# Slot weights turned in two passes and spread by transfers, a centring matrix, and values weighed in three rounded passes

## What is computed

```python
Q = xn @ Wq + bq                                   # layer 0, per sequence of 512
probs = softmax(Q @ Q.T / sqrt(128));  s = probs @ Q
logits = (xn @ phi_w.T + phi_b).reshape(t, z, 64, 32)
D = softmax(logits, axis=slots);  C = softmax(logits, axis=experts)
X = layernorm(einsum('tznp,tzd->npd', D, xn));  Y = tanh(X) @ expert_w + expert_b
g = silu(einsum('tznp,npH->tzH', C, Y));  x = x + s * g
xn = layernorm(x)                                  # layer 1
h_t = a_t * h_(t-1) + gated_t;  s = rmsnorm(h) @ W_out.T
k = relu(xk @ W_k.T)**2;  r = sigmoid(xr @ W_r.T);  g = silu(r * (k @ W_v.T));  x = x + s * g
```

## Time and profile before

| | |
|---|---|
| runs | 1345.48, 1346.94, 1347.56 us (median 1346.94) |
| the profiled execution | 1348.3 us, its span 1346.2 us |
| PE busy | 1252.0 us (93%) |
| DVE, ACT, POOL busy | 1051.1, 740.2, 814.2 us (78%, 55%, 60%) |
| mean granted clock of TensorE | 0.98 |
| DMA | 167.35 MB, mean 124 GB/s |

### The profile page before, as it was taken

The page is one execution under the profiler, slowest core; times in us unless marked ns, Lnnn a source line. Parts: engine busy times, 40 slices in busy tenths (PEclk is TensorE's granted clock), DMA queues, the critical chain, the costliest instruction groups (busy, mean ns, idle before and its releaser), DMA issues.

```text
span 1346.2 us, 17623 instructions
## 1 busy us (share of the span) xinstructions
PE 1252.0 (93%) x4866; PEld 740.7 (55%) x4866; DVE 1051.1 (78%) x1533; ACT 740.2 (55%) x1459; POOL 814.2 (60%) x768
## 2 busy tenths in 40 slices
PE   6699999999999999998699999999999999999984
PEld 2465555555555555553465555665555565555641
DVE  6899999999999999996455777666776667776653
ACT  2655556556665555653434555555655555655554
POOL 3588989999898898996244454343453344453320
PEclk9899999999999999999799999999999999999997
DMA  6433333333333333333643333333333333333310
GB/s 199 120 139 124 141 128 137 140 125 140 134 131 141 124 140 131 134 141 141 196 133 118 102 125 117 111 125 110 118 123 105 125 118 110 117 110 125 125 32 16
DMA packets 123217, 167.35 MB, mean 124 GB/s; under 512 B 7153, under 2 KB 99313, under 8 KB 122993
## 3 DMA queue, kind: packets, MB, share of 16 engines
q1 hardware_dynamic: 122688, 164.65, 35.5%
q10 hardware_dynamic: 434, 1.59, 0.4%
HBM read 90.71 MB, written 75.50 MB: 123 GB/s over the span
## 4 chain that ended last, share of the span: by engine, by line
PE 37%; POOL 5%; DVE 4%; issue 4%; ACT 0%; POOLq 0%; DVEq 0%
PE yac L797 12%; PE ct L785 6%; POOL b_e L1331 5%; PE at L854 4%; PE at L844 2%; DVE nmx L1180 2%; PE lp L894 1%; PE lp L906 1%; PE lp L900 1%; DVE b_ti L1259 1%; PE lp L139 1%; PE lp L869 1%; PE at L830 1%; PE at L833 1%; PE at L832 1%
## 5 line engine op out<-in xcount | busy, mean ns | idle before, releaser
L562 POOL TENSOR_TENSOR dd<-ed,rz 128x512 f32<-128x512 f32 x256 | 263.4, 1050 | 58.9 <-DVE rz L551 58.9
L463 PE MATMUL acc<-dd,xns 128*128 128x512 f32 x512 | 260.9, 592 | 1.3 <-POOL dd L562 1.3
L797 PE MATMUL yac<-cf,expert_out 128*128 128x512 f32 x512 | 261.7, 594 | 0.0
L1167 DVE TENSOR_TENSOR cf<-ct,slot_weight 128x512 f32<-128x512 f32 x256 | 175.3, 685 | 87.1 <-PE ct L785 84.1
L498 ACT ACTIVATE ed<-lg 128x512 f32<-128x512 f32 x256 | 138.9, 595 | 84.7 <-PE lg L448 84.7
L538 DVE TENSOR_REDUCE mr<-lg 128x32 fp32r<-128x1024 f32 x128 | 154.6, 1208 | 26.0 <-PE lg L434 26.0
L785 PEld LDWEIGHTS ct<-identity,exp_slots_loaded 128*128 128x128 f32 x1024 | 127.7, 142 | 80.1 <-issue 67.3
L570 POOL TENSOR_TENSOR slot_weight<-exp_slots_loaded 128x512 f32<-128x512 f32 x128 | 164.5, 1286 | 0.0
L432 PE MATMUL lg<-phi_transposed,xn_transposed 128*128 128x512 f32 x256 | 158.4, 619 | 2.2 <-PEq L359 1.8
L504 ACT ACTIVATE exp_slots_loaded<-lg 128x512 f32<-128x512 f32 x256 | 139.0, 595 | 30.3 <-PE lg L454 30.2
L546 DVE TENSOR_REDUCE zd<-ed 128x32 f32<-128x1024 f32 x128 | 154.8, 1209 | 1.0 <-ACT ed L498 1.0
(11 more groups left out here) (187 smaller groups left out, 2242.0 us busy)
## 6 DMA issues: line engine op xcount, KB each, us to landing
exp_slots<-exp_slots_loaded SPq DMA_DIRECT2D x128, 512.0 KB, 2.7
exp_slots_loaded<-exp_slots SPq DMA_DIRECT2D x128, 512.0 KB, 3.4
xns<-xn_rows SPq DMA_DIRECT2D x128, 64.0 KB, 1.7
expert_w<-in_expert_w SPq DMA_DIRECT2D x8, 512.0 KB, 5.3
b_xraw<-in_xT SPq DMA_DIRECT2D x16, 256.0 KB, 3.7
out_t<-b_ti SPq DMA_DIRECT2D x16, 256.0 KB, 4.1
xn_rows<-slot_max SPq DMA_DIRECT2D x2, 1024.0 KB, 5.1
xn_rows<-slot_sum SPq DMA_DIRECT2D x2, 1024.0 KB, 5.3
```

The source lines that it names most:

```text
L463: e.matmul(acc[k][:, :], xns[w % RX][:, :], dd[w % RX][:, bank(k)], start=tile == 0, stop=tile == NT - 1, skip_group_check=True).then_inc( ...
L562: e.tensor_tensor(dd[v % RX][:, bank(k)].rearrange("q (n p) -> q n p", p=NP), ed[c][:, bank(k)].rearrange("q (n p) -> q n p", p=NP), rz[c] ...
L797: e.matmul(yac[:, :], YF[:, c, :], cf[c % RC][:, :], start=c == 0, stop=c == CH - 1).then_inc(c_y)
L1167: e.tensor_tensor(cf[c % RC][:, :], ct[c % 2][:, :], WT[i % 2][c // (CH // HALVES)][:, :], ALU.mult).then_inc(c_w)
```

## The change

In words, by place. **First half:** `slot_max` and `slot_sum` are no longer kept in SBUF for the second half but stored to DRAM (`slot_statistics`), most of it by SP during the first half (four transfers at units 70 and 118), the last 16 tiles in the middle stage. **Middle stage and second half:** the statistics of a sequence come back by two transfers (`join_load`); `join_weights` makes 128x256 numbers instead of 128x1024; `join_turned` turns two tiles instead of eight, into `lp1` alone; ACT copies 128x256; SP stores that to DRAM and loads it back eight times, so that each of the four groups of 32 partitions gets its copy (`join_stored`, `join_spread`). The join's steps stand earlier in an iteration. **Layer 1's norm:** `mean` multiplies by `identity_minus_mean`, so its product is already centred; `centre` goes, and `squares` and `normalise` read PSUM. **Attention:** Q's and the values' rounded parts come from ACT, `value_low` and `turn_low` (DVE) make remainders, and `weigh` is three float32r products instead of one float32 product. **Moved:** `weighted_rows` from POOL to ACT; the rounding of xn from DVE to ACT; k squared from ACT to POOL; `mix` from `difference` (POOL). **Gone:** the copies `yt` and `x1k`. Without `yt`, the accumulator `yac` is free only after DVE's `silu_y`.

```diff
         def join_weights(e, b):
             e.wait_ge(s_wv, WV * b + 2)
             if b:
-                e.wait_ge(s_wt, HALVES * b)
+                e.wait_ge(s_wt, b)
+            e.tensor_tensor(WR[:, :, :, :], MS[:, :, :, :], both_halves(MJ[:, :, :]), ALU.mult).then_inc(s_wp)
+
+        def join_turned(e, b, out):
+            e.wait_ge(s_wp, WP * (b + 1))
             for h in range(HALVES):
-                e.tensor_tensor(WR[:, h], joined(SM, b)[:, h].unsqueeze(2).broadcast_to([P, TPB, EPC, NP]),
-                                MJ[:, :, :].unsqueeze(2).broadcast_to([P, TPB, EPC, NP]), ALU.mult).then_inc(s_wp)
-
-        def join_turned(e, b, h, out):
-            e.wait_ge(s_wp, WP * (b + 1))
-            for k in range(TPB):
-                done = e.transpose(out[:, k * TILE:(k + 1) * TILE], WR[:, h, k, :, :].rearrange("q j p -> q (j p)"), IDENT[:, :])
+                done = e.transpose(out[:, h * TILE:(h + 1) * TILE], WR[:, h, :, :].rearrange("q t p -> q (t p)"), IDENT[:, :])
             done.then_inc(s_wt)
 
-        def join_copied(e, b, h, out):
-            e.wait_ge(s_wt, HALVES * b + h + 1)
-            e.activation(WT[b % 2][h][:, :], out[:, :], ACT.Copy).then_inc(s_wc)
+        def join_copied(e, b, out):
+            e.wait_ge(s_wt, b + 1)
+            if b:
+                e.wait_ge(s_wd, 16 * b)
+            e.activation(WS[:, :, :].rearrange("r h k -> r (h k)"), out[:, 0:HALVES * TILE], ACT.Copy).then_inc(s_wc)
+
+        def join_stored(e, b):
+            e.wait_ge(s_wc, b + 1)
+            if b >= 2:
+                e.wait_ge(s_wl, 16 * WL * (b - 1))
+            e.dma_start(WD[b % 2].rearrange("h r k -> r h k"), WS[:, :, :]).then_inc(s_wd, 16)
+
+        def join_spread(e, b):
+            e.wait_ge(s_wd, 16 * (b + 1))
+            for j in range(EPC):
+                for h in range(HALVES):
+                    e.dma_start(WT[b % 2][j * NP:(j + 1) * NP, h, :].rearrange("p (t k) -> p t k", t=TPB),
+                                WD[b % 2][h].rearrange("(t p) k -> p t k", p=NP)).then_inc(s_wl, 16)
...
+                    if v == NT + 6:
+                        e.wait_ge(s_sm, NT)
+                        e.dma_start(STATS[:, 0, 0, :, :], SM[:, 0, :, :]).then_inc(s_stat, 16)
+                        e.wait_ge(s_ss, NT // TPB)
+                        e.dma_start(STATS[:, 1, 0, :, :], SS[:, 0, :, :]).then_inc(s_stat, 16)
...
+                e.wait_ge(s_stat, 64)
+                join_load(e, 0)
+                for k, src in ((0, SM), (1, SS)):
+                    e.dma_start(STATS[:, k, 1, EARLY:NT, :], src[:, 1, EARLY:NT, :]).then_inc(s_stat, 16)
                 for k in range(RE):
-                    e.wait_ge(s_est[k], 16 * (UNITS // RE))
+                    e.wait_ge(s_exp[k], STORED)
                 for g in range(RL):
                     load_exps(e, g)
+                join_stored(e, 0)
+                join_spread(e, 0)
+                join_load(e, 1)
                 for g in range(RW, GROUPS):
                     e.wait_ge(s_yf, (g - RW + 1) * CPG)
                     load_experts(g)
+                e.wait_ge(s_stat, 96)
...
+                        if k == 3 and i + 1 < NB:
+                            join_stored(e, i + 1)
+                        if k == 4 and i + 1 < NB:
+                            if i:
+                                e.wait_ge(c_w, i * CH)
+                            join_spread(e, i + 1)
...
-                        e.matmul(lp[0][:, :], MEAN[:, :], B["x1"][:, :], start=True, stop=True).then_inc(S["mn"])
+                        e.matmul(lp[0][:, :], CENTRE[:, :], B[f"x1{i % 2}"][:, :], start=True, stop=True).then_inc(S["mn"])
...
                     if c == 0 and i:
-                        e.wait_ge(y_c, i)
-                    e.matmul(yac[:, :], YF[:, c, :], cf[c % RC][:, :], start=c == 0, stop=c == CH - 1).then_inc(c_y)
+                        e.wait_ge(S["u_y"], i)
+                    e.matmul(yac[:, :], YF[:, c, :], cf[g % RF][:, :], start=c == 0, stop=c == CH - 1).then_inc(c_y)
...
-                    e.matmul(at[0][:, :], B["vf"][:, rows(k)], pt[k % 2][:, :], start=k == 0, stop=k == TPB - 1).then_inc(A["w"])
+                        e.wait_ge(S["v_l"], i + 1)
+                    e.matmul(at[0][:, :], R["vh"][:, rows(k)], pth[k % 2][:, :], start=k == 0, stop=False)
+                    e.matmul(at[0][:, :], R["vl"][:, rows(k)], pth[k % 2][:, :], start=False, stop=False)
+                    e.wait_ge(A["kl"], i * TPB + k + 1)
+                    e.matmul(at[0][:, :], R["vh"][:, rows(k)], ptl[k % 2][:, :], start=False, stop=k == TPB - 1).then_inc(A["w"])
...
                         e.wait_ge(S["ix"], i + 1)
+                        e.wait_ge(s_wc, min(i + 4, NB))
                         e.matmul(lp[1][:, :], MEAN[:, :], B["a2"][:, :], start=True, stop=True).then_inc(S["hm"])
...
+                        if c == 5:
+                            weighted_rows(i, 0)
+                        if c == 6:
+                            weighted_rows(i, 1)
+                            if i + 1 < NB:
+                                join_copied(e, i + 1, lp[1])
                         if c == 7:
+                            weighted_rows(i, 2)
+                            weighted_rows(i, 3)
                             squares(i - 1)
...
+                        e.scalar_tensor_tensor(B["ty"][:, :], B["ty"][:, :], 1.0, yac[:, :], ALU.add, ALU.mult).then_inc(S["u_y"])
...
+                def turn_low(i, k):
+                    if within(i):
+                        e.wait_ge(A["kh"], i * TPB + k + 1)
+                        e.tensor_tensor(ptl[k % 2][:, :], at[1][:, :], hi_f32(pth[k % 2][:, :]), ALU.subtract).then_inc(A["kl"])
...
+                        if c in (9, 11, 13, 15):
+                            turn_low(i, (c - 9) // 2)
                         if c == 4:
                             weights(i, 0)
+                            if i + 1 < NB:
+                                join_inverse(e, i + 1)
```

More of the change, by code:

```diff
@@ L415, in sync1 @@
                     if v == 0:
[L416 to L417 removed]
+                        e.wait_ge(s_xnd, 64)
                     if v >= RX:
@@ L666, in scalar1b @@
                     e.activation(XTT[:, bank(q)], xc[:, bank(q)], ACT.Tanh).then_inc(s_th)
-                for h in range(HALVES):
-                    join_copied(e, 0, h, pw[h])
             def vector1b(e):
@@ L1145, in scalar2 @@
                             state_squares(i - 2)
-                        if c == 9 and within(i - 1):
-                            e.preload_act_table_set("exp_and_others")
-                        if c == 11:
-                            if i + 1 < NB:
-                                for h in range(HALVES):
-                                    join_copied(e, i + 1, h, lp[h])
                         if c == 12:
@@ L1312, in vector2 @@
                             scan(i - 2)
-                        if c == 6:
-                            centre(i - 1)
-                        if c == 7 and i + 1 < NB:
-                            join_inverse(e, i + 1)
                         if c == 9:
```

344 lines of the change are left out of this document (173 added, 171 removed), and 4 rows, old and new, of the table S.

## The result

The changed kernel takes 1369.49 us in the median (1368.78 to 1370.08), beside 1347.25 us (1345.48 to 1348.34) for the kernel before: a ratio of 1.0166, interval 1.0148 to 1.0184. It is slower, by 22 us where 8 were forecast. The profiled span goes from 1346.2 to 1368.3 us.

What follows compares the result with a forecast made beforehand. PE's order was taken as the clock of the second half. 1346.9 + 8.7 (middle stage) + 1.8 (thirteen periods) - 2.2 (first and last iterations, drain) = 1355 us; the 8-in-10 range ran from 1341 to 1370.

Steps and rivals of the forecast that it cites:

- The work on PE: Second half, per iteration: PE's work falls from 38.85 to 37.52 us through `weigh` (0.68) and slot weights (0.65).
- Wait 1: Opening product of step 3: PE now waits for DVE's `silu_y`, 1.13 us per iteration, new.
- Wait 3: `state_mean`: PE waits 1.37 us per iteration for `join_copied`, behind the second `weighted_rows` on ACT.
- Wait 2: Slot-weight turns ahead of step 5: PE waits 0.73 us per iteration for POOL's 128x256 product.
- Wait 4: `weigh` k = 1: rounding and remainders come late, 0.2 us per iteration on PE; bounds 0 and 1.2.
- The middle stage: Late statistics and expert loads behind the spread start the second half +8.7 us later; bounds +3.4 and +11.
- the queue: Middle stage, SP: statistics load waits behind expert loads, lands about 647.3, moving `join_max` by 7.4 us.
- The rival with the load landing by itself: Middle stage costs only +3.4, second half as forecast: 1348 to 1350 us; chance 0.12.
- Iterations 0 and 1: Start of the second half: less work and no POOL wait, against new waits: -1.45 and -0.32 us.
- The drain: End of the second half: one ACT copy goes, k squared is slower on POOL, about even; iteration 15 -0.4.
- rival of 1335 us: Second half: new waits replace the old 1.96 us instead of adding, period 39.5 us, faster; chance 0.15.
- The rival of 1370 us: Second half: `turn_low` waits for ACT, each of k = 0 to 3 costing PE 0.3; period 42.0; chance 0.20.

Runs made afterwards that it cites:

- Experiment 10: Changed kernel with ACT's copy `yt` back and `join_copied` ahead of the second `weighted_rows`; 1334.00 us, ratio 0.9891.
- Experiment 1: Changed kernel with ACT's copy of `yac` into `yt` restored, so the opening product waits for that copy alone; 1348.84 us, ratio 1.0006.
- Experiment 7: Kernel before, with its opening product of step 3 waiting for DVE's `silu_y`, `yt` still made; 1368.80 us, ratio 1.0151.
- Experiment 2: Changed kernel with `join_copied` ahead of the second `weighted_rows` on ACT; 1352.41 us, ratio 1.0025.
- experiment 5: Changed kernel with the statistics load ahead of the first expert loads on SP in the middle stage; 1365.66 us, ratio 1.0122.
- experiment 6: Kernel of experiment 5 with the last four expert loads also ahead of the store and the spread; 1363.51 us, ratio 1.0111.
- Experiment 3: Changed kernel with PE's slot-weight turns one step later; 1378.37 us, ratio 1.0213.
- Experiment 4: Kernel of Experiment 3 with `mean` issued twice into the same bank, the first product useless; 1369.69 us, ratio 1.0151.

## Why the prediction was right in direction and too small

**The work on PE** was as forecast. Period less waits is 41.78 - 4.23 = 37.55 us in the changed kernel; 37.52 was the term. Experiment 10, with Waits 1 and 3 gone, bears both out: 41.78 - 1.45 - 1.32 = 39.01, and its period is 39.00.

**The sum of the waits** is the step that failed: forecast 1.13 + 0.73 + 1.37 + 0.20 = 3.43, measured in the chain 1.45 + 0.99 + 1.32 + 0.47 = 4.23 us. That makes +0.97 per period out of +0.14, and 12.5 us out of 1.8 in thirteen of them: 10.7 us, by far the largest part of the 14 us by which the forecast was short.
- *Wait 1*, 1.45 for 1.13. The stop is 1.23: the handoff from DVE to PE takes 0.13 (917.04 to 917.17), where I took 0.05. Behind it comes what the prediction lacked altogether, the restart, 1.10 for 0.86. Experiments 1 and 7 show the term at 1.45 and 1.28.
- *Wait 2*, 0.99 for 0.73, in the same way: stop 0.81, restart 0.19. POOL's product takes 0.73, where 0.74 was taken from the earlier trace rows.
- *Wait 3*, 1.32 for 1.37. Two misses cancel: PE comes 0.26 later out of Wait 2, so it waits less, and pays its restart. Experiment 2 gives back 1.26.
- *Wait 4*, 0.47 for 0.20, inside the bounds of 0 and 1.2. It is at the place named, `weigh` k = 1, and the remainder is one of its two causes.

The restart could have been read: the product behind the wait for ACT is busy for 1.13 in the earlier trace rows price such a product at 0.86. I priced each product by the distance of starts elsewhere and each wait by its idle time, and so lost 0.2 to 0.24 us at each.

**The residual** on DVE was expected to be relieved of POOL, and was; this row answers to the earlier trace rows:

```profile
L1271 DVE SCALAR_TENSOR_TENSOR b_x<-b_ty,b_xraw x16: 691/693/694, 716.7 to 1330.7; 128x512 f32<-128x512 f32 x16
```

693 ns in the median where there were 1162, and from it to step 5's product 924.71 - 922.18 = 2.53 us, the number taken. The Trainium skill, "SBUF — State Buffer" ("Who interferes with whom"), says that a DVE operation with two SBUF inputs and a POOL operation that reads SBUF get in each other's way. The trace agrees: in the iteration shown POOL has no instruction between 921.64 and the end of the residual.

**The middle stage** was +8.7 in the forecast and +11.4 in the trace. Its first step, the queue, held: `join_max` at 647.8 for 647.3 forecast, and experiment 5 moved it to 641.0 by the load's place in the queue alone. The rival with the load landing by itself fell. With the rule of the Trainium skill, "DMA: Bandwidth & Descriptors" ("Queues, rings and completion order"), that a DMA engine takes the descriptors of a ring in order, the trace agrees. The terms behind it were too small: the last expert loads are issued at 664.4 and not 662.6, of which 1.0 us is the eight spreading issues (3.66 us, 0.46 each, where 0.33 was taken) and 0.5 the later `join_max`; and the second half starts 10.7 us after them instead of 9.7. By the seven experiments with this stage unedited the start is 9.9 to 12.6 us later than before, above the forecast in each.

**Iterations 0 and 1** were -1.8 in the forecast and are -3.7. Of the missing 1.9, 1.05 us is the clock up to Q of iteration 0, which comes 2.38 us behind the start of the second half in the kernel before and 1.33 in the changed one. The windows of the first 5 us, before and after:

```profile
663.60:668.60 5.00, 4.98 (x20) 4.28 (x21) 2.01 (x5) 1.37 (x3) 2.00 (x2) 0.50 0.09 27
```

```profile
675.00:680.00 5.00, 4.01 (x26) 3.18 (x27) 3.12 (x7) 3.45 (x5) 2.92 (x4) 1.00 0.32 105
```

That is luck of this one execution and no gain of the change: in the seven experiments that leave the middle stage alone the granted clock of these 5 us is 0.50 to 0.70, and Q comes 2.4 us behind the start, as in the kernel before. Experiment 5 (0.67) has the 2.4 too, which is why its start, 4.9 us earlier, was worth only 3.8 in the span. The other 0.8 lies in iteration 0 and is not the clock: from Q to Q it takes 30.09 us here and 30.05 to 30.08 in experiments 1, 2, 5 and 6, which entered at the lower clock. Its cause stays open.

**The drain** was about even in the forecast, with -0.4 for iteration 15, and is +1.9. Two rows of it:

```profile
1337.64 1.91 PE L924 MATMUL lp<-b_ty,ones_over_width 128*128 128x512 f32 x2
```

```profile
1340.96 1.28 ACT L1189 ACT_TABLE_LOAD   x1
1342.25 0.63 ACT L1061 ACTIVATE r_xh<-xn 128x512 fp32r<-128x512 f32 x1
```

The variance product is still at half clock and takes 1.91 us, where it took 1.02 before; and the rounding of xn, moved from DVE to ACT, stands behind a table load, so that POOL gets it 1.30 us after xn is done and not 0.55. No experiment was made for these two. But experiments 3 and 4 differ by the second `mean` alone, and from Q of iteration 15 to the end they take 80.4 and 78.3 us; the variance product takes 1.91 in the one and 1.10 in the other. The second `mean` fills the stop there, so stop and clock of the drain are worth 2.1 us between these two, enough for the whole 1.9; what the rounding adds stays open.

The second half's rival of 1335 us was to decide from less than 2.6 us of waits; there are 4.23. Experiment 10 runs at 1334 us, but that isn't this rival come true: its period is 39.0 and not 39.5, because Waits 1 and 3 are taken out, and its second half starts 12.6 us later than before and not 8.7. The rival of 1370 us, DVE late throughout, meets the measured time, and that is luck: it had 0.3 us at each of the four `weigh`, where the chain has 0.47 at k = 1 and nothing at the others, and most of the loss is in Waits 1 and 2 and their restarts.

## What to carry to other kernels

Removing work from an engine that has time to spare can cost far more than it saves, if that work released a resource of the engine that has none: a copy out of PSUM of 0.6 us was worth 21 us. Before deleting a copy, ask who waits for the buffer that it frees. When work is taken from the bounding engine, list every release that it will now reach earlier, and price each stop with its restart; what stands ahead of the releasing instruction in its own stream is the first thing to change. And a wait can't be mended by moving only the waiting instruction: undo the producer's delay first, then move (the same move cost 0.93 us before and gave 0.14 after).

## What the runs showed of the hardware that was not expected

- A float32 product of 512 columns behind a stop of 1.1 to 1.2 us costs 1.10 us, 0.86 in a row; two transposes 0.41 instead of 0.22. The first recurs in every kernel here that stops there, also behind a stop of 0.54 us.
- Behind stops of 2.09 us, in every second iteration, TensorE was granted 1.2 GHz for some 3 us; behind the stops of up to 1.23 us in the changed kernel's loop it stayed at 2.4 GHz (1.00 in the windows). With useless work in front of the stop the kernel became 8.7 us faster.
- The granted clock of the first 5 us of the second half was 1.00 in one execution of the changed kernel and 0.50 to 0.70 in the seven experiments with the same middle stage. The full clock gave 1.05 us, and one profile doesn't tell that it will be there.
- One transfer issue on SP took 0.46 us in the spread, and 3.2 us for the first statistics load, issued right behind eight large loads.
